# Latent attention in a fused Perceiver block: scores of two heads together, rotary products side by side, and a pipeline one head longer

## What is computed

```python
qc = x @ W_D_Q;  c = x @ W_D_KV
q_base = (qc @ W_U_Q).reshape(B, L, 16, 128);  q_rope = _rope((qc @ W_Q_R).reshape(B, L, 16, 64))
k_base = (c @ W_U_K).reshape(B, L, 16, 128);   k_rope = _rope((x @ W_K_R).reshape(B, L, 16, 64))
v = (c @ W_U_V).reshape(B, L, 16, 128)
scores = einsum('bqhd,bkhd->bhqk', [q_base q_rope], [k_base k_rope]) * 128 ** -0.5
out = einsum('bhqk,bkhd->bqhd', softmax(scores), v).reshape(B, L, 2048) @ W_O
```

## Time and profile before

| what | value |
|---|---|
| median of 3 runs (lowest to highest) | 676.11 us (675.7 to 680.04) |
| the profiled execution, its own time | 676.34 us |
| its span | 674.6 us, 10704 instructions |
| PE busy | 572.1 us, 85% |
| DVE busy | 497.8 us, 74% |
| ACT busy | 365.4 us, 54% |
| POOL busy | 44.6 us, 7% |
| chain that ended last | PE 42%, DVE 23%, issue 18%, ACT 15%, DMA 2% |

### The profile page before, as it was taken

The page is one execution under the profiler, slowest core; times in us unless marked ns, Lnnn a source line. Parts: engine busy times, 40 slices in busy tenths (PEclk is TensorE's granted clock), DMA queues, the critical chain, the costliest instruction groups (busy, mean ns, idle before and its releaser), DMA issues.

```text
span 674.6 us, 10704 instructions
## 1 busy us (share of the span) xinstructions
PE 572.1 (85%) x4315; PEld 358.4 (53%) x4318; DVE 497.8 (74%) x894; ACT 365.4 (54%) x389; POOL 44.6 (7%) x30
## 2 busy tenths in 40 slices
PE   2899999976999599959995886799999999964667
PEld 2345555434555455545553655488884555532364
DVE  2599999676899779987998795201664773699985
ACT  5525746464798579957995785201126246432233
POOL 0200000000000000000000000000000000026860
PEclk9999999996999699969996675899999999996879
DMA  9423200260335234423343599000607404010000
GB/s 325 179 76 113 62 1 1 74 224 1 125 143 165 69 126 127 165 86 126 125 149 103 212 321 408 4 1 1 249 1 297 200 14 175 0 62 1 0 1 31
DMA packets 18896, 76.67 MB, mean 114 GB/s; under 512 B 1952, under 2 KB 3104, under 8 KB 16800
## 3 DMA queue, kind: packets, MB, share of 16 engines
q1 hardware_dynamic: 18848, 76.00, 31.5%
HBM read 75.20 MB, written 0.79 MB: 113 GB/s over the span
## 4 chain that ended last, share of the span: by engine, by line
PE 42%; DVE 23%; issue 18%; ACT 15%; DMA 2%; SPq 0%; ACTq 0%; DVEq 0%
PE ps L703 10%; PE ps L573 6%; ACT arena L1376 4%; PE ps L531 3%; PE ps L762 3%; ACT arena L1369 3%; DVE arena L933 3%; DVE arena L940 3%; PE ps L729 3%; DVE arena L924 3%; ACT arena L1362 3%; PE ps L728 2%; ACT arena L1341 2%; PE ps L747 2%; PE ps L541 2%
## 5 line engine op out<-in xcount | busy, mean ns | idle before, releaser
L1010 DVE CUSTOM_DVE_ANT_0 arena<-ps,arena 128x1024 f32<-128x1024 f32 x128 | 153.8, 1218 | 23.9 <-PE ps L560 16.4
L1369 ACT ACTIVATE arena<-arena,small 128x4096 int16<-128x4096 f32 x32 | 121.7, 3803 | 0.0
L573 PE MATMUL ps<-small,arena 128*128 128x128 bf16 x1024 | 91.8, 242 | 17.2 <-ACT arena L1369 17.1
L531 PE MATMUL ps<-arena 128*128 128x512 f16 x384 | 101.8, 390 | 0.0
L497 PE MATMUL ps<-arena 128*128 128x512 f16 x384 | 85.2, 379 | 0.9 <-DVE arena L933 0.9
L573 PEld LDWEIGHTS ps<-small,arena 128*128 128x128 bf16 x1024 | 68.5, 108 | 27.2 <-ACT arena L1369 19.8
L1376 ACT ACTIVATE arena<-ps 128x1024 bf16<-128x1024 int16 x64 | 65.3, 1024 | 27.2 <-PE ps L573 26.8
L703 PE MATMUL ps<-arena 128*128 128x256 f32 (+1 forms) x288 | 68.7, 398 | 0.7 <-ACT arena L1442 0.7
L588 PEld LDWEIGHTS ps<-arena 128*128 128x128 bf16 x1024 | 43.7, 100 | 38.4 <-issue 10.1
L703 PEld LDWEIGHTS ps<-arena 128*128 128x128 f32 x288 | 55.8, 194 | 11.8 <-issue 3.3
L497 PEld LDWEIGHTS ps<-arena 128*128 128x128 f16 x384 | 37.2, 98 | 43.3 <-issue 1.3
(11 more groups left out here) (152 smaller groups left out, 818.0 us busy)
## 6 DMA issues: line engine op xcount, KB each, us to landing
arena<-key_scales SPq DMA_DIRECT2D x64, 512.0 KB, 5.2
arena<-in_ctxT SPq DMA_DIRECT2D x8, 1024.0 KB, 5.5
arena<-in_wg SPq DMA_DIRECT2D x1, 4096.0 KB, 12.1
arena<-in_wo SPq DMA_DIRECT2D x1, 4096.0 KB, 12.0
arena<-in_wu SPq DMA_DIRECT2D x1, 4096.0 KB, 21.4
arena<-in_wd SPq DMA_DIRECT2D x4, 1024.0 KB, 6.1
arena<-in_wuq SPq DMA_DIRECT2D x1, 3072.0 KB, 22.8
arena<-in_wkr SPq DMA_DIRECT2D x1, 2048.0 KB, 12.1
```

Source lines behind the costliest of these rows:

```text
L531: last = pe.matmul(ps[:, bank, :], wv16[wpart][:, k, g * P:(g + 1) * P], ctx16[cpart][:, k, tok], start=(k == 0 and i == 0), stop=(k == KC ...
L573: last = pe.transpose(ps[:, bank, :].bitcast(BF16)[:, b * P:(b + 1) * P], p16[u % 2][:, (8 * q + b) * P:(8 * q + b + 1) * P].bitcast(BF16) ...
L1010: dve.tensor_tensor_reduce(sc[:, u % 2, i * SCW:(i + 1) * SCW], ps[:, 2 * (n % 2):2 * (n % 2) + 2, :].rearrange("p a b -> p (a b)"), skb[: ...
L1369: act.activation(p16[u % 2], sc[:, u % 2, :], ACT.Exp, bias=ebias[:, u % 2:u % 2 + 1], scale=sq[:, i:i + 1], accum_out=rsum[:, u:u + 1]).t ...
```

## The change

On PE one call of `scores2` now makes the scores of heads h and h+1. For each query tile it makes the two products with 128 rows, one for each head and bank, and then the two rotary products, which use partitions 0 to 63 and 64 to 127. The call stands in even steps alone and waits for the exponentials of both heads before. Turns, values and projections follow one step later than before: `turn2(i-2)`, `values2(i-3)`, `project2(i-4)`, and the loop has one step more. On DVE the copy of the values follows for head i-3, and the ternary steps are 4 to 9 and 14 to 19. On ACT the copy of the turned probabilities is now that of head i-2 and stands ahead of the exponentials of step i; `abs_sum` keeps its step numbers. No operation is added or left out.

```diff
             def scores2(h):
                 if h == 0:
                     pe.wait_ge(rpu, NROPE)
-                if h >= 2:
-                    pe.wait_ge(ex2, h - 1)
-                a = DR * (h % 2)
+                else:
+                    pe.wait_ge(ex2, h)
                 for t in range(QT):
-                    o = ps[:, h % 2, t * N:(t + 1) * N]
                     q = slice(t * P, (t + 1) * P)
-                    pe.matmul(o, qbT[:, h, q], kbT[:, h, :], start=True, stop=False)
-                    last = pe.matmul(o, qrT[a:a + DR, h // 2, q], krT[a:a + DR, h // 2, :], start=False, stop=True)
-                last.then_inc(sc2, 1)
+                    for b in range(2):
+                        pe.matmul(ps[:, b, t * N:(t + 1) * N], qbT[:, h + b, q], kbT[:, h + b, :],
+                                  start=True, stop=False)
+                    for b in range(2):
+                        a = slice(DR * b, DR * (b + 1))
+                        last = pe.matmul(ps[:, b, t * N:(t + 1) * N], qrT[a, h // 2, q], krT[a, h // 2, :],
+                                         start=False, stop=True)
+                        if t == QT - 1:
+                            last.then_inc(sc2, 1)
...
-            for i in range(NH + 3):
-                if i < NH:
+            for i in range(NH + 4):
+                if i < NH and i % 2 == 0:
                     scores2(i)
-                if 0 <= i - 1 < NH:
-                    turn2(i - 1)
-                if 0 <= i - 2 < NH:
-                    values2(i - 2)
-                if i == NH + 2:
+                if 0 <= i - 2 < NH:
+                    turn2(i - 2)
+                if 0 <= i - 3 < NH:
+                    values2(i - 3)
+                if i == NH + 3:
                     pe.wait_ge(wgs, 12)
...
-                if 0 <= i - 3 < NH:
-                    project2(i - 3)
+                if 0 <= i - 4 < NH:
+                    project2(i - 4)
...
             def tern_at(i):
-                return i - 3 if 3 <= i < 9 else i - 7 if 13 <= i < 19 else None
+                return i - 4 if 4 <= i < 10 else i - 8 if 14 <= i < 20 else None
...
-                h = i - 2
+                h = i - 3
                 if 0 <= h < NH:
                     dve.wait_ge(av2, h + 1)
...
-            for i in range(NH + 1):
-                if i < NH:
-                    act.wait_ge(nb2, i + 1)
-                    if i >= 2:
-                        act.wait_ge(pt2, i - 1)
-                    for t in range(QT):
-                        ins = act.activation(e2[:, i % 2, t, :], ps[:, i % 2, t * N:(t + 1) * N], ACT.Exp,
...
-                h = i - 1
+            for i in range(NH + 2):
+                h = i - 2
                 if h >= 0:
                     act.wait_ge(pt2, h + 1)
                     if h >= 2:
                         act.wait_ge(av2, h - 1)
                     act.activation(pT2[:, h % 2, :, :], ps[:, 2 + h % 2, :].rearrange("p (a b) -> p a b", a=QT),
                                    ACT.Copy).then_inc(pe2, 1)
+                if i < NH:
+                    act.wait_ge(nb2, i + 1)
+                    for t in range(QT):
+                        ins = act.activation(e2[:, i % 2, t, :], ps[:, i % 2, t * N:(t + 1) * N], ACT.Exp,
...
                 if i < 2:
                     abs_sum(wg32[:, 2 + i, :], 2 + i)
```

More of the change, by code:

```diff
@@ L1459, in _ @@
                     abs_sum(wg32[:, (n - V0 + 2) // 2, :], (n - V0 + 2) // 2)
-            for i in range(NH + 1):
-                if i < NH:
-                    act.wait_ge(nb2, i + 1)
-                    if i >= 2:
-                        act.wait_ge(pt2, i - 1)
-                    for t in range(QT):
-                        ins = act.activation(e2[:, i % 2, t, :], ps[:, i % 2, t * N:(t + 1) * N], ACT.Exp,
-                                             bias=nmax2[:, i % 2, t:t + 1], scale=DH ** -0.5,
-                                             accum_out=sum2[:, i % 2, t:t + 1])
-                    ins.then_inc(ex2, 1)
-                h = i - 1
+            for i in range(NH + 2):
+                h = i - 2
                 if h >= 0:
@@ L1476, in _ @@
                                    ACT.Copy).then_inc(pe2, 1)
+                if i < NH:
+                    act.wait_ge(nb2, i + 1)
+                    for t in range(QT):
+                        ins = act.activation(e2[:, i % 2, t, :], ps[:, i % 2, t * N:(t + 1) * N], ACT.Exp,
+                                             bias=nmax2[:, i % 2, t:t + 1], scale=DH ** -0.5,
+                                             accum_out=sum2[:, i % 2, t:t + 1])
+                    ins.then_inc(ex2, 1)
                 if i < 2:
```

## The result

The changed kernel takes 683.05 us (median of 5 runs, 682.39 to 684.71). Beside it the kernel before took 677.44 (median of 5). The ratio is 1.0087, with a 95% interval from 1.0064 to 1.011: 0.9% slower, inside the 1% that I had called no change, and 0.7 us from the forecast of 682.4. The number was right. One step behind it was not, and another was too small; that they cancelled was luck.

The account below looks back on a forecast made before the run. PE was taken to bound the middle of the loop, DVE and the last load its end; 3.1 us at the end, 1.0 and 2.0 for half clock, on 676.34, gave 682.4 us, range 676.5 to 687.5.

Parts of the forecast that it names:

- What bounds the loop: Whole loop: PE, busy 30.00 of 30.00 us from 530 to 560, bounds the middle; DVE and the last load the end.
- Price of the scores: Scores on PE: a pair of heads falls from 4.82 to 3.7 us (3.3 to 4.1), with 0.2 per change.
- at best three pass times of 0.215, 0.65: Rotary pair on PE: second head's first pass lies at best beside the first head's second pass, so 0.65 us.
- my first rival: Scores on PE: rotary products lie wholly beside each other, same half clock; +4.2 us, 680.5; chance 0.13.
- some 0.65 us between starts: Sign of being right: the pair of L732 rotary products on PE shows some 0.65 us between starts.
- The wait at the start: Loop start: PE waits for exponentials 4.7 us before scores 2 and 2.5 us before scores 4.
- the last term of that chain: Loop start: ACT's sum of absolute values, about 1.9 us, stands ahead of exponential 1, which starts at 518.2.
- The half clock: PE after its long waits: half clock costs 2.0 us from the start and 1.0 us at the end.
- The middle: Steady pairs of heads: 9.84 us of PE against 10.98; scores 14 start near 577.2 against 581.5.
- The end: Loop end: ACT's sum, waiting for the load, delays the copy of head 15; end 3.1 us later, PE idle 6.8.
- The sum: Whole kernel: +3.1 + 1.0 + 2.0 = 6.1 us, added to 676.34, gives 682.4.
- the case in which the changes vanish too: Scores on PE: full overlap, clock holds and no cost for changes of height; 670.6 us, chance 0.06.

Follow-up runs that it names:

- e2_own: Changed kernel with the products of a head pair in their old order, head by head, base and rotary in turn, none side by side: 696.44 us, ratio 1.0301.
- e3_alone: Changed kernel with, head by head, two base products and then two rotary products, so that no rotary products overlap: 692.83 us, ratio 1.0229.
- e1_tail: Changed kernel with ACT's sum over the last quarter of the third matrix moved behind the copy of head 15: 677.73 us, ratio 1.0023.
- e7_start: Changed kernel with DVE's odd-head maximum ahead of the even head's normalisation and ACT's step-0 sum moved behind exponential 1: 676.52 us, ratio 0.9993.
- e13_fill_tail: e1_tail plus 10 unused PE products ahead of the wait of scores 2: 674.65 us, ratio 0.9967.
- e4_four: Changed kernel with all four base products of a pair ahead of its four rotary products, two changes of height instead of four: 676.62 us, ratio 0.999.
- e6_fill: Changed kernel plus unused PE products, 10 ahead of the wait of scores 2 and 14 ahead of that of values 15: 680.3 us, ratio 1.0046.

## Why the prediction was right, and where it was not

- **What bounds the loop**: right. PE in the middle, but for a wait of a quarter of a microsecond in most pairs (e2_own, e3_alone), the order on DVE and ACT at the ends (e1_tail, e7_start).
- **Price of the scores**: a change of height at 0.2 us was right (0.80 for four, e3_alone against e2_own). The step "at best three pass times of 0.215, 0.65" failed. Two rotary products lie wholly over each other: the pair of scores is 3.2 us, not 3.7, and e3_alone gives the 0.86 us that two hidden products are worth. I had reasoned that the second head's first pass must start behind the first head's second pass; the trace shows the four passes of L732 in one row that is as long as the two passes of L729 alone (0.70 us, below). This was the mechanism of my first rival, to which I gave 0.13. The sign that I had named, "some 0.65 us between starts", does not tell the two apart: the 0.63 us measured between starts are 0.43 for the products and 0.20 for a change of height.
- **The wait at the start**: right, 4.83 and 2.37 us for 4.7 and 2.5. What was put beside it was right in sum only: the last term of that chain is DVE's second maximum as much as ACT's sum.
- **The half clock**: right that it comes after the wait at the start and after the one at the end. Mis-sized is the term of 2.0 us at the start. The first alone costs 2.4 (e13_fill_tail). A second one, which I did not have, follows the second wait, from 530.7 to 534; a pair of scores took 5.0 us there instead of 3.2, another 1.8. The 1.8 are read from the rows; e4_four, which has no half clock there, gained 1.9 us beyond its seven distances. That is about 4 us for 2.
- **The middle**: 9.64 us a pair where 9.84 was worked out: the scores are 0.5 us cheaper, and 0.27 of that went into the wait for the exponential.
- **The end**: right. The eighteenth ternary operation was due 83.2 us into the loop with the start's clock, and the load was asked for at 83.1. From there to the residual add were 14.7 us forecast and 14.3 measured; the load took 4.9 instead of 5.3.
- **The sum**: loop 98.0 forecast, 97.4 measured. Scores 14 started 68.8 us into the loop, and my layout with its 2.0 us for the half clock had 68.3. Up to there it had some 1.7 us too much, since the rotary pairs were cheaper (less what went into waits), and 2.2 too little for the half clock. So the errors cancelled, which was luck. The 1.0 us more behind the loop is no effect of the change that can be told from noise: that stretch took 71.2 to 73.0 us over the profiles of all kernels, whatever their loop. Two sums do not come out as written, without consequence: the layouts of the end differ by 605.8 - 602.55 = 3.25 us, not 3.1, and the case in which the changes vanish too is 676.1 - 3.5 = 672.6, not 670.6, which lies outside the range all the same. The rival whose mechanism came true carried 680.5, 2.5 below the measurement, because it had the same half clock too cheap.

## What to carry to other kernels

When steps of a pipeline are moved, follow on every engine each instruction that waits for something slow, and ask what now stands behind it: one copy behind a sum that waits for a load cost 5.6 us here, as much as the whole loss. Work that is issued for two items together needs the results of both, so the first rounds, which have nothing to put in between, pay for the whole chain, and PE pays again through its clock. The same edit can gain with one distance and lose with another (e7's order of maximum and normalisation), so reorder for the result that is waited for in that layout.

## What the runs showed of the hardware that I had not expected

Float32 products of 64 rows in different row groups overlap with both of their passes. The row of the changed kernel's timeline, four MATMULs (two products), and the row behind it:

```profile
541.80 0.70 PE L732 MATMUL ps<-arena 64*128 64x256 f32 x4
542.43 1.13 PE L728 MATMUL ps<-arena 128*128 128x256 f32 x4
```

It is as long as the two MATMULs of one product at 559.90, and PE goes on after 0.63 us where it was 0.62 there. Of its four MATMULs two start at 541.80 and two at 542.12: the first passes of both heads run together, then the second ones. The rule of the Trainium skill that the prediction had set aside for float32 (TensorE: Matmul & The Clock Gate, Part 3) holds here: the pack takes the time of one, within 0.01 us.

The half clock did not follow the length of the wait. Behind a wait of 4.8 us it lasted 5 us of busy PE in the changed kernel; behind one of 2.7 us in e3_alone it lasted for 24 us of busy PE, from 519.0 to 530.0 and from 532.4 to 545.7. The second wait, 2.37 us, was followed by a half clock in the changed kernel and by the full clock in e4_four. What decides it, these runs do not show.

The last load, of 1 MB, took 4.7 to 5.3 us from issue to its reader's start in 13 of the 14 profiles and 7.2 us in one (e6_fill).
